# One gather of a token's normed row, shared result and sum, instead of three

## The reference, cut to what matters

```
h   = layernorm(x)                                    # the normed row
sh  = ln(silu(h @ sw1.T + sb1) * (h @ sw2.T + sb2))
shared_out = sh @ sw3.T + sb3                         # the shared result
x_moe = h[index_b, index_t]                           # 1024 chosen tokens
top1  = argmax(sigmoid(x_moe @ eg_w.T + eg_b) + exp_bias)
w     = softmax([shared_score, top1_score])
z     = ln(silu(x_moe @ ew1[top1].T + ..) * (x_moe @ ew2[top1].T + ..))
out   = shared_out, and at the chosen tokens  w[0] * shared_out + w[1] * (z @ ew3[top1].T + ..)
x     = x + out
```

## Time and profile before

| | us |
|---|---|
| median of 3 runs | 3115.16 |
| lowest, highest | 3112.65, 3118.74 |
| the profiled execution, its own time | 3110.86 |
| its span | 3108.7 |

### The profile page before, as it was taken

The page is one execution under the profiler, slowest core; times in us unless marked ns, Lnnn a source line. Parts: engine busy times, 40 slices in busy tenths (PEclk is TensorE's granted clock), DMA queues, the critical chain, the costliest instruction groups (busy, mean ns, idle before and its releaser), DMA issues. The chain is left out here.

```text
span 3108.7 us, 41598 instructions
## 1 busy us (share of the span) xinstructions
PE 2907.8 (94%) x15224; PEld 1723.7 (55%) x15224; DVE 2079.6 (67%) x3794; ACT 1608.4 (52%) x2998; POOL 1738.8 (56%) x747
## 2 busy tenths in 40 slices
PE   8999799999999999999999999979969997999577
PEld 5888455555555555555555555437845553777433
DVE  4332587777777777777777777635638896677423
ACT  2222066666676666667676776733216674222211
POOL 0000178989898989898989898830020101334366
PEclk9999599999999999999999999989979998999789
DMA  7544835465566565665655656356665563333451
GB/s 228 184 173 152 217 80 119 96 141 129 118 137 130 119 136 113 133 133 113 140 127 120 131 114 145 79 136 199 191 154 142 142 161 114 138 135 109 150 181 41
DMA packets 179536, 427.52 MB, mean 138 GB/s; under 512 B 30189, under 2 KB 51598, under 8 KB 156236
## 3 DMA queue, kind: packets, MB, share of 16 engines
q1 hardware_dynamic: 153158, 275.92, 30.7%
q0 software_dynamic: 24288, 145.27, 22.6%
q10 hardware_dynamic: 1888, 3.67, 0.3%
HBM read 180.69 MB, written 118.79 MB: 96 GB/s over the span
## 5 line engine op out<-in xcount | busy, mean ns | idle before, releaser
L825 DVE TENSOR_REDUCE part_max<-ps_s 128x1 f32<-128x512 f32 x2048 | 1270.6, 683 | 369.2 <-PE ps_s L713 369.1
L925 ACT ACTIVATE probs<-ps_st 128x512 f32<-128x512 f32 x2048 | 1057.9, 602 | 491.5 <-PE ps_st L732 481.9
L660 POOL TENSOR_TENSOR added<-added,probs 128x2048 f32<-128x2048 f32 x251 | 1168.3, 4654 | 72.0 <-ACT probs L925 48.8
L732 PE MATMUL ps_st<-q_stack,k_stack 98*128 98x512 f32 x2048 | 864.7, 425 | 10.4 <-ACT probs L925 9.1
L713 PE MATMUL ps_s<-k_stack,q_stack 96*128 96x512 f32 x2048 | 826.5, 410 | 16.8 <-DMA k_stack<-k_lo 16.8
L732 PEld LDWEIGHTS ps_st<-q_stack,k_stack 98*128 98x128 f32 x2048 | 386.6, 189 | 518.8 <-ACT probs L925 369.3
L743 PE MATMUL ps_pv<-probs,v_sb 128*32 128x512 f32 x4096 | 546.6, 606 | 0.0
L713 PEld LDWEIGHTS ps_s<-k_stack,q_stack 96*128 96x128 f32 x2048 | 396.1, 194 | 111.5 <-DVE part_max L825 30.9
L668 POOL DMA_DIRECT2D probs<-probs x128 | 110.8, 866 | 181.2 <-PE ps_pv L743 176.7
L743 PEld LDWEIGHTS ps_pv<-probs,v_sb 128*32 128x32 f32 x4096 | 80.7, 108 | 162.8 <-ACT probs L925 136.5
L660 POOL TENSOR_TENSOR added<-probs 128x2048 f32<-128x2048 f32 x32 | 146.7, 4583 | 10.4 <-ACT probs L925 10.2
(11 more groups left out here) (286 smaller groups left out, 3543.4 us busy)
## 6 DMA issues: line engine op xcount, KB each, us to landing
probs<-probs POOLq DMA_DIRECT2D x128, 1024.0 KB, 7.1
q_stack<-q_hi SPq DMA_DIRECT2D x64, 256.0 KB, 6.1
k_stack<-k_hi SPq DMA_DIRECT2D x64, 256.0 KB, 5.7
xq_stack<-q_parts SPq DMA_DIRECT2D x32, 512.0 KB, 5.0
q_parts<-k_stack SPq DMA_DIRECT2D x60, 256.0 KB, 3.9
x_in<-in_x_rows SPq DMA_DIRECT2D x8, 1024.0 KB, 8.2
q_hi<-qk_h_out SPq DMA_DIRECT2D x8, 1024.0 KB
q_lo<-qk_l_out SPq DMA_DIRECT2D x8, 1024.0 KB, 6.2
```

Of the source, the lines that this page charges most:

```text
L660: pool.tensor_tensor(added[:, w % 2], left, probs[:, k % RING], ALU.add).then_inc(added_up, 1)
L732: pe.matmul(ps_st[:, n % BANKS], k_stack[0:TOP, w // BPB, j, k * P:(k + 1) * P], q_stack[:, w % 4, j], start=True, stop=True).then_inc(ite ...
L825: dve.tensor_reduce(part_max[:, s:s + 1], ps_s[:, (w * SLOTS + s) % BANKS], AX.X, ALU.max)\
L925: act.activation(probs[:, k % RING, j], ps_st[:, n % BANKS], ACT.Exp, scale=SCALE).then_inc(item_used, 1)
```

## The change

`h_rows` stays for the choice of experts. `shared_rows` is replaced by `token_rows`, a DRAM array with 6 KB a token: normed row, shared result and sum side by side. SyncE stores the normed rows twice (to `h_rows` and to `token_rows`), the shared result once, and the sum twice (to `out_rows` and to `token_rows`); each of the stores into `token_rows` writes 2 KB pieces at a pitch of 6 KB. The semaphores count accordingly. In `selected_experts` one gather of 6 KB rows takes the place of three gathers of 2 KB rows; the three buffers are 6 KB a slot, and only they are cleared (`acc` isn't any more). The gather of tile s + 3 also waits until the sum of tile s is lessened. Since scatters no longer touch what the gathers read, the scatter of tile s - 2 follows in step s from s = 2 on.

```
             sp.dma_start(h_blocks[2 * i + u], h_out[:, u]).then_inc(h_stored[u], 16)
+            sp.dma_start(normed_blocks[2 * i + u], h_out[:, u]).then_inc(h_stored[u], 16)
...
             sp.dma_start(out_blocks[2 * i + u], out_sb[:]).then_inc(out_stored, 16)
+            sp.dma_start(sum_blocks[2 * i + u], out_sb[:]).then_inc(out_stored, 16)
...
-        h_in = sb("h_in", [P, RING, D])
-        shared_in = sb("shared_in", [P, 2, D])
+        rows_in = sb("rows_in", [P, RING, 3, D])
...
                         if s >= RING:
                             pool.wait_ge(xt_in_psum, s - RING + 1)
-                        pool.indirect_dma_start(h_in[:, s % RING], None, h_rows, rows_of(s),
+                            pool.wait_ge(lessened, s - RING + 1)
+                        pool.indirect_dma_start(rows_in[:, s % RING].rearrange("p n d -> p (n d)"), None, token_rows, rows_of(s),
...
-                pool.wait_ge(cleared, 1)
                 pool.wait_ge(slots_loaded, 16)
-                gather_tile(0)
-                gather_tile(1)
-                pool.wait_ge(cleared, 3)
-                gather_shared(0)
-                gather_out(0)
-                gather_tile(2)
-                gather_out(1)
-                gather_out(2)
-                gather_shared(1)
+                for s in range(RING):
+                    pool.wait_ge(cleared, s + 1)
+                    gather_tile(s)
...
                     gather_tile(s + RING)
-                    gather_shared(s + 2)
-                    for _ in range(3):
-                        if out_to_come:
-                            gather_out(out_to_come.pop(0))
-                    if not out_to_come and s > 5:
-                        if not sent:
-                            for t in range(TILES):
-                                pool.wait_ge(out_gathered[t], 16)
-                        while sent < min(s - 1, 2 * (s - 5)):
-                            scatter(sent)
-                            sent += 1
+                    if s >= 2:
+                        scatter(s - 2)
...
-                dve.memset(h_in[:], 0.0).then_inc(cleared, 1)
-                dve.memset(shared_in[:], 0.0).then_inc(cleared, 1)
-                dve.memset(acc[:], 0.0).then_inc(cleared, 1)
+                for s in range(RING):
+                    dve.memset(rows_in[:, s], 0.0).then_inc(cleared, 1)
...
-                        dve.wait_ge(shared_gathered[s % 2], 16 * (s // 2 + 1))
-                        dve.wait_ge(out_gathered[s], 16)
-                        dve.scalar_tensor_tensor(out=acc[:, s], in0=shared_in[:, s % 2], scalar=slots[:, s, 2:3],
-                                                 in1=acc[:, s], op0=ALU.mult, op1=ALU.add).then_inc(lessened, 1)
+                        dve.wait_ge(tile_gathered[s % RING], 16 * (s // RING + 1))
+                        dve.scalar_tensor_tensor(out=acc[:, s], in0=rows_in[:, s % RING, 1], scalar=slots[:, s, 2:3],
+                                                 in1=rows_in[:, s % RING, 2], op0=ALU.mult, op1=ALU.add).then_inc(lessened, 1)
```

More of the change, by code:

```diff
@@ L1741, in shared_feed_forward @@
         blocks_of = lambda rows: rows.rearrange("(n t p) d -> n p t d", t=TPB, p=P)
-        x1_blocks, h_blocks, shared_blocks, out_blocks = (blocks_of(r) for r in (x1_rows, h_rows, shared_rows, out_rows))
+        x1_blocks, h_blocks, out_blocks = (blocks_of(r) for r in (x1_rows, h_rows, out_rows))
+        normed_blocks, shared_blocks, sum_blocks = (blocks_of(token_rows[:, n * D:(n + 1) * D]) for n in range(3))
         a_blocks = attn_t.rearrange("b (c p) (n k) -> b n p c k", p=P, k=BLK)
@@ L1980, in output @@
                     if t == 0 and not first(i, u):
-                        dve.wait_ge(out_stored, count(i, u, 16, 0))
+                        dve.wait_ge(out_stored, count(i, u, 32, 0))
                     dve.tensor_tensor(out_sb[:, t], ps_f[:, t % 2], x2[:, u, t], ALU.add).then_inc(out_done, 1)
@@ L2334, in _, with selected_experts @@
                 blocks(pe, body)
-def selected_experts(nc, h_rows, shared_rows, out_rows, tile_ends, table_scattered, w12_t, w3_t, bias, gamma, beta, eye,
+def selected_experts(nc, token_rows, out_rows, tile_ends, table_scattered, w12_t, w3_t, bias, gamma, beta, eye,
                      ramp, slot_table):
@@ L2446, in _ @@
                 pool.wait_ge(consts, 2)
-                pool.wait_ge(cleared, 1)
                 pool.wait_ge(slots_loaded, 16)
-                gather_tile(0)
-                gather_tile(1)
-                pool.wait_ge(cleared, 3)
-                gather_shared(0)
-                gather_out(0)
-                gather_tile(2)
-                gather_out(1)
-                gather_out(2)
-                gather_shared(1)
+                for s in range(RING):
+                    pool.wait_ge(cleared, s + 1)
+                    gather_tile(s)
                 pool.wait_ge(small_loaded, 16 * SMALL)
-                out_to_come = list(range(3, TILES))
-                sent = 0
                 for s in range(TILES):
@@ L2469, in _ @@
                     gather_tile(s + RING)
-                    gather_shared(s + 2)
-                    for _ in range(3):
-                        if out_to_come:
-                            gather_out(out_to_come.pop(0))
-                    if not out_to_come and s > 5:
-                        if not sent:
-                            for t in range(TILES):
-                                pool.wait_ge(out_gathered[t], 16)
-                        while sent < min(s - 1, 2 * (s - 5)):
-                            scatter(sent)
-                            sent += 1
-                for s in range(sent, TILES):
+                    if s >= 2:
+                        scatter(s - 2)
+                for s in range(TILES - 2, TILES):
                     scatter(s)
@@ L2575, in tile_in @@
                         for c in range(DC):
-                            mm = pe.transpose(ps_t[:, s % 2, c], h_in[:, s % RING, c * P:(c + 1) * P], ident[:])
+                            mm = pe.transpose(ps_t[:, s % 2, c], rows_in[:, s % RING, 0, c * P:(c + 1) * P], ident[:])
                         mm.then_inc(xt_in_psum, 1)
```

28 lines of the change are left out of this document (8 added, 20 removed).

## The result

The changed kernel took 3124.7 us (median of 8 runs, 3118.34 to 3130.29) where the kernel before took 3115.59 (median of 8, 3112.65 to 3128.49). The ratio is 1.0027, 95% interval 1.0014 to 1.0040: slower, by 8.4 us (4.4 to 12.5). The prediction was 3119, +4.2, with 3109 to 3128 as its range. One execution of an experiment, 6618.65 us at a mean granted clock of 0.397, is left out of its ratio.

What follows compares the result with a forecast made beforehand. TensorE at 94% of the span, but in the last stage gather landing decides its waits. Loop +0.3, start +0.8, shared stage's end +2.6, last block +0.5: +4.2, 3115.1 for the profiled execution, 3119 for the median; range 3109 to 3128.

Steps and rivals of the forecast that it cites:

- within 0.2%: Whole kernel: change of under about 6.2 us, not told from no change; chance 0.50, against slower 0.38 and faster 0.12.
- signs of being wrong: Full tiles landing below 4 or above 6 us, clock falling twice or never, or stores costing more than 4 us.
- GpSimd's queue: Last stage: 30 of 60 indirect DMAs remain, the root is never late again, gathers always issue 5.14 us behind their silu.
- The landing: Last stage's 6 KB gathers: full tiles land in 4.9 us, tiles of 3 to 14 tokens 2.7, empty ones 2.2.
- The loop: Last stage, silu of tile 3 to 14: waits of 9.6 us in all, 89.0 against 91.98, -3.0 at full clock.
- one stretch of slow clock at least stays: -3.0 + 3.3 = +0.3: Last stage's loop: waits of 2.8, 2.8 and 2.2 us still cause one TensorE fall to 1.2 GHz, costing 3.3 us.
- the clock decides: Rival, last stage's loop: two or three long waits drop TensorE to 1.2 GHz, 3122.7 or 3126.0 us; chance 0.33.
- Start of the stage, +0.8: Last stage: first result shifts by 3.3 us, tile 3's gather then lands faster, +0.8 is left; ends -0.5 and +3.
- End of the shared stage, +2.6: Another 1 MB of stores behind the sums, with nothing to hide it: +2.6 us; ends 1.5 and 4.5.
- The last block: Shared stage: gather of chosen rows waits for 1 MB more of stores, 2.6 us, mostly hidden: +0.5; ends 0 and 2.6.
- The end of the kernel: Behind the last scatter: it hangs on TensorE's last sum, so scatters sent earlier shorten nothing: 0.

## Why the prediction was right or wrong

Its range for 8 in 10 held the time, and its direction was right, but its likeliest case, "within 0.2%", was not what came, and the time lies just above the forecast's own range of 3114 to 3124. Two of its signs of being wrong did come: with this loop the clock fell never in two profiles and twice or three times in three others, and what the stores touch, the last block and the end of the shared stage, cost 6.0 by the table (4.8 if the last block counts 3.2, as worked out above) instead of at most 4. That the range held is partly luck. By the table the last block is 3.9 above its term, the loop 3.9 and the start of the stage 2.1; the end of the shared stage is 1.0 below, and the 2.5 at the kernel's end, which the prediction doesn't have, hide a part of the rest. Point by point:

- **GpSimd's queue: right.** No root of the loop is late (the one of tile 1, ahead of it, starts right behind a gather at 2987.96), and a gather is issued 5.12 or 5.13 behind its silu, as the 5.14 that I used.
- **The landing: right, at its upper edge.** 5.0 to 5.5 against my 4.9 (4.6 to 5.3). By the Trainium skill ("DMA: Bandwidth & Descriptors", "Anatomy of one DMA") the estimate was 3.8; the trace disagrees, with 5.0 to 5.5. Tiles with few tokens were undersized: up to 3.8, not 2.7, which makes waits at tiles 9 to 11 of 0.5 to 1.0.
- **The loop: the waits right, the clock wrong.** Waits of 2.97, 2.55 and 2.20 where I had 2.8, 2.8 and 2.2, and 10.8 in all against 9.6. The step that failed is "one stretch of slow clock at least stays: -3.0 + 3.3 = +0.3". The number of stretches is not the kernel's but the execution's: none in two profiles with this loop, two in two and three in one, so +4.2 in the mean instead of +0.3. My rival "the clock decides" described the longer executions, and I weighed the two as exclusive where they were a mixture: +4.2 for the whole could be the kernel's median only if one stretch were usual. The Trainium skill ("TensorE: Matmul & The Clock Gate", "HAM oscillation — how this bites in real kernels") tells of a kernel that fell at each of its waits, which are longer than these and stand between shorter bursts of matmuls; the profile with three falls agrees with a fall at each long wait, the changed kernel's own, with none, does not.
- **Start of the stage, +0.8: mis-sized.** It is 2.5 to S(0), less than the 3.3 that I had for the shift, but nothing of it is hidden at tile 3: to S(3) it is 2.9. That tile 3's gather would land in 2.2 to 2.7 once the weights are in was wrong. It was issued at 2986.76, which is 22.6 behind the stage's first gather where it was 20.9, and still took 5.20; in another profile it took 4.4.
- **End of the shared stage, +2.6:** 1.6 in the mean, 2.4 in the profiled execution. But the account was wrong: with the output's last store no longer awaited, the stage ends at the same time. What it waits for is open.
- **The last block, "I take +0.5, most of it hidden by those; ends 0 and 2.6": failed.** By the table it is +4.4, and +3.9 (or 3.2) with more executions of either kind, above my upper end of 2.6. The gather of the chosen rows starts 3.6 nearer to the last long matmuls (3.98 ahead of them, not 7.55), not 2.6. The cover that I named was the root with its 1.10 of idle time; but the path runs through TensorE's transposes of the chosen rows, whose 2.3 us of wait nothing hides. I also left the clock out: those small matmuls take 1.40 us a tile at one level and 2.45 at the other, and where the clock falls among them moved the stretch by 4 us between two executions of one kernel. That the store moves this fall is likely but not shown.
- **The end of the kernel: not seen.** "What is sent earlier shortens nothing at the end" is true, but that fewer are sent does: -2.5.

## What to carry to other kernels

Before merging transfers, ask whether the longer one is still hidden: here the change lost 8 us with three buffers, its stores included, and with a fourth it became the better design by about 4 us (0.9962 against 0.9975; the intervals overlap). Price a wait in front of small matmuls with the clock that it may cost, and when a stretch of slow clock is near its edge, profile more than one execution before you give it a number. A second store of data that is at hand anyway is not free where a gather waits on the same semaphore.

## What the runs showed of the hardware

- Two executions with like waits (2.63 and 2.97 us) take different levels of TensorE's clock behind them; over all the profiles, waits of 1.72 to 3.2 us in the loop went either way (1.72 was followed by a fall in one, 1.77 by none in another), and waits up to 1.53 us were never followed by one.
- With no wait left in the loop, three kernels spread over 4.0 us (3097.41 to 3101.44), 5.1 and 7.3 in five timed runs each, where the changed kernel's eight spread over 12.
- Ending the last stage takes longer when GpSimd has issued 60 indirect DMAs in it than with 30: 8.6 against 6.0 us behind the start of the last scatter, while 12 or 17 more semaphores cost 0.15.
- Gathers of 128 rows: 2 KB rows land in 3.4, 6 KB rows in 5.0 to 5.5, none in 2.2; with 14 tokens 2.7 and 3.8; among expert weights at about 400 GB/s, 8.5 us for 6 KB rows and 5.9 for 2 KB rows.
